# Cross-attention and FFN layers on one core: the router's product in 8 passes of 16 columns instead of 12 of 8

## What is computed

```
def _L1_ffn_ref(hidden_states, router_weight, sh_gate, sh_up, sh_down, r_gate, r_up, r_down):
    ...
    x = hidden_states.reshape(-1, H)
    logits = x.astype(jnp.float32) @ router_weight.astype(jnp.float32).T
    topk_vals, topk_idx = jax.lax.top_k(logits, TOP_K)
    topk_w = jax.nn.softmax(topk_vals, axis=-1)
    slot_mask = (topk_idx < NUM_LOCAL).astype(topk_w.dtype)
    comb_w = jnp.sum(topk_w * slot_mask, axis=-1).astype(x.dtype)
    shared = _mlp(x, sh_gate, sh_up, sh_down)
    routed = _mlp(x, r_gate, r_up, r_down) * comb_w[:, None]
    return (shared + routed).reshape(Bsz, Seq, H)
```

## Time and profile before

| | us |
|---|---|
| median of 3 runs | 455.13 |
| the 3 runs | 454.22, 456.38, 455.13 |
| the profiled execution | 456.1 |
| its span, first to last instruction | 454.4 |

### The profile page before, as it was taken

The page is one execution under the profiler, slowest core; times in us unless marked ns, Lnnn a source line. Parts: engine busy times, 40 slices in busy tenths (PEclk is TensorE's granted clock), DMA queues, the critical chain, the costliest instruction groups (busy, mean ns, idle before and its releaser), DMA issues.

```text
span 454.4 us, 8501 instructions
## 1 busy us (share of the span) xinstructions
PE 395.8 (87%) x3034; PEld 370.1 (81%) x3034; DVE 308.2 (68%) x929; ACT 226.6 (50%) x622; POOL 182.2 (40%) x300
## 2 busy tenths in 40 slices
PE   0668747699998999999989999999899989998596
PEld 0546636599987998899979997999789979996495
DVE  3479767796786666878765758878665666765343
ACT  0285564456564344656644345656543456564132
POOL 2235283734553433455434334545533332322031
PEclk9988986899999999999999999999999999999699
DMA  7997001000000001100000002000000000000000
GB/s 212 364 343 282 1 0 50 1 2 1 1 0 3 0 1 30 45 1 1 2 1 1 1 1 72 2 1 2 1 1 2 1 23 1 2 2 0 0 1 23
DMA packets 15080, 16.85 MB, mean 37 GB/s; under 512 B 1536, under 2 KB 14016, under 8 KB 15040
## 3 DMA queue, kind: packets, MB, share of 16 engines
q1 hardware_dynamic: 15040, 16.33, 11.1%
HBM read 15.28 MB, written 1.05 MB: 36 GB/s over the span
## 4 chain that ended last, share of the span: by engine, by line
PE 50%; DVE 24%; ACT 12%; POOL 6%; issue 5%; DMA 2%; SPq 1%; DVEq 0%; POOLq 0%; ACTq 0%
PE bank_s L300 13%; PE bank_u L300 10%; PE bank_qa L300 6%; ACT prob L741 6%; DVE prob L1326 5%; PE bank_o L300 4%; PE bank_pt L300 4%; PE bank_pt L471 3%; DVE pt_lo L1337 3%; DVE xn L1140 2%; POOL prob L1000 2%; DVE ut_lo L1343 2%; DMA wq_raw<-in_wqT 2%; ACT ut_hi L707 2%; PE bank_s L568 2%
## 5 line engine op out<-in xcount | busy, mean ns | idle before, releaser
L1000 POOL TENSOR_SCALAR prob<-prob,row_inv,valid_b 128x256 f32<-128x256 f32 x128 | 71.5, 567 | 84.2 <-DVE row_inv L1333 83.6
L741 ACT ACTIVATE prob<-prob,row_min 128x256 f32<-128x256 f32 x128 | 64.1, 502 | 71.5 <-DVE row_min L1326 71.5
L1337 DVE TENSOR_TENSOR pt_lo<-bank_pt,pt_hi 128x512 fp32r<-128x512 f32 x64 | 44.2, 690 | 14.1 <-ACT pt_hi L707 13.8
L1343 DVE TENSOR_TENSOR ut_lo<-bank_u,ut_hi 128x256 fp32r<-128x256 f32 x64 | 27.0, 422 | 38.6 <-ACT ut_hi L707 38.2
L1326 DVE CUSTOM_DVE_ANT_0 prob<-bank_s,masked 128x256 f32<-128x256 f32 x128 | 48.9, 419 | 2.9 <-PE bank_s L300 2.3
L300 PE MATMUL bank_u<-pt_hi,cx_hi 128*128 128x256 f32 x128 | 37.8, 295 | 7.0 <-DVE pt_lo L1337 6.7
L1012 POOL TENSOR_TENSOR act_lo<-act_raw,act_hi 128x256 fp32r<-128x256 f32 x32 | 24.0, 749 | 48.0 <-ACT act_hi L800 48.0
L300 PE MATMUL bank_o<-c_hi,ut_hi 128*128 128x256 f32 x128 | 39.2, 306 | 4.5 <-DVE ut_lo L1343 4.5
L707 ACT ACTIVATE pt_hi<-bank_pt 128x512 fp32r<-128x512 f32 x64 | 37.5, 586 | 10.8 <-PE bank_pt L471 10.8
L471 PE MATMUL bank_pt<-ident,prob 128*128 128x128 f32 x256 | 39.4, 277 | 3.9 <-POOL prob L1000 3.6
L300 PE MATMUL bank_qa<-xt_hi,a_hi 128*128 128x256 f32 x128 | 41.0, 320 | 0.8 <-DVE qa_lo L1315 0.7
(11 more groups left out here) (234 smaller groups left out, 1300.7 us busy)
## 6 DMA issues: line engine op xcount, KB each, us to landing
wq_raw<-in_wqT SPq DMA_DIRECT2D x4, 512.0 KB, 8.8
wo_raw<-in_wo SPq DMA_DIRECT2D x4, 512.0 KB, 9.7
w_raw<-in_w12T SPq DMA_DIRECT2D x1, 1408.0 KB, 9.1
gate_raw<-in_gateT SPq DMA_DIRECT2D x2, 576.0 KB, 8.8
up_raw<-in_upT SPq DMA_DIRECT2D x2, 576.0 KB, 10.5
down_raw<-in_downT SPq DMA_DIRECT2D x2, 576.0 KB, 12.4
x<-in_x SPq DMA_DIRECT2D x4, 256.0 KB, 5.3
guT<-in_guT SPq DMA_DIRECT2D x4, 256.0 KB, 6.8
```

What stands on the lines that cost most here:

```text
L741: last = act.activation(row, row, ACT.Exp, scale=-1.0, bias=row_min[:, h % 2, t:t + 1], accum_out=row_sum[:, h % 2, t:t + 1])
L1000: last = pool.tensor_scalar(row, row, row_inv[:, h % 2, t:t + 1], valid_b[:, 0:1], ALU.mult, ALU.mult)
L1337: dve.tensor_tensor(pt_lo[:, :, :].rearrange("p s t -> p (s t)"), bank["pt"][:, :], f32(pt_hi[:, :, :].rearrange("p s t -> p (s t)")), ALU ...
L1343: dve.tensor_tensor(ut_lo[:, :], bank["u"][:, 0:T], f32(ut_hi[:, :]), ALU.subtract).then_inc(S["u_l"], 1)
```

## The change

The two parts of the router's weights lie side by side in one tile, 8 columns of the high and 8 of the low. One pass multiplies a block of rows by all 16, so that a block needs two passes (its high and its low part) and not three; per batch 8 and not 12. The low by low product, left out before, is included. A row group's result has 16 columns in the bank: the sum of what met the high weights and the sum of what met the low. VectorE copies the first 8 to SBUF, adds the other 8, and takes the maxima from the sum. The NOP at that place is gone.

```diff
-        router_hi = sb("router_hi", [P, ND, NR], F32R)
-        router_lo = sb("router_lo", [P, ND, NR], F32R)
+        router = sb("router", [P, ND, 2, NR], F32R)
...
+        logits = sb("logits", [P, NT, NR])
...
                 for t in range(NT):
+                    cols = slice(t * P, (t + 1) * P)
                     for k in range(ND):
-                        cols = slice(t * P, (t + 1) * P)
-                        last = split_mm(bank["x1"][:, t * NR:(t + 1) * NR], yt_hi[:, k, cols], yt_lo[:, k, cols],
-                                        router_hi[:, k, :], router_lo[:, k, :], k == 0, k == ND - 1)
+                        for half in (yt_hi, yt_lo):
+                            last = pe.matmul(bank["x1"][:, t * 2 * NR:(t + 1) * 2 * NR], half[:, k, cols],
+                                             router[:, k, :, :].rearrange("p s n -> p (s n)"),
+                                             start=(k == 0 and half is yt_hi), stop=(k == ND - 1 and half is yt_lo),
+                                             skip_group_check=True)
                 last.then_inc(S["route_mm"], 1)
...
-            act.copy(router_hi[:, :, :], router_raw[:, :, :]).then_inc(S["router_hi"], 1)
+            act.copy(router[:, :, 0, :], router_raw[:, :, :]).then_inc(S["router_hi"], 1)
...
                 dve.wait_ge(S["route_mm"], b + 1)
-                hold()
-                for t in range(NT):
-                    last = dve.max(top8[:, t, :], bank["x1"][:, t * NR:(t + 1) * NR])
+                parts = bank["x1"][:, 0:NT * 2 * NR].rearrange("p (t s n) -> p s t n", s=2, n=NR)
+                link(dve.tensor_copy(top8[:, :, :], parts[:, 0, :, :]))
+                link(dve.tensor_tensor(logits[:, :, :], top8[:, :, :], parts[:, 1, :, :], ALU.add))
+                for t in range(NT):
+                    last = dve.max(top8[:, t, :], logits[:, t, :])
                 link(last)
...
-            dve.tensor_tensor(router_lo[:, :, :], router_raw[:, :, :], f32(router_hi[:, :, :]), ALU.subtract
+            dve.tensor_tensor(router[:, :, 1, :], router_raw[:, :, :], f32(router[:, :, 0, :]), ALU.subtract
                               ).then_inc(S["router_lo"], 1)
```

## The result

| | before | with the change |
|---|---|---|
| median | 456.38 | 458.37 |
| fastest run | 453.94 | 455.79 |
| profiled execution | 456.1 | 457.04 |
| its span | 454.4 | 455.1 |
| mean granted clock in it | 0.966 | 0.968 |

Both medians are of 13 runs on one chip; one run of each kernel (1309 and 2079 us) is left out of the comparison. The ratio is 1.0044, 95% interval 1.0022 to 1.0065. That is 2.0 us (458.37 - 456.38). It lies inside the 0.5% that the forecast called no change, but the interval leaves no doubt of its sign, and 458.37 lies above the forecast's range (453.3 to 456.9). Part of that distance, 1.25 us, is the kernel before itself, whose median was 455.13 in the three runs that the forecast started from. But a difference of 0.0 was forecast, and 2.0 came.

A forecast was written before the change was run, and what follows sets the result against it. TensorE, back to back, bounds the kernel, closely followed by a relay over VectorE, ScalarE and GpSimd. 3 x 0.15 - 0.45 = 0.0 us, so 455.1 against the 455.13 median (profiled 456.1); range 453.3 to 456.9.

The forecast's parts named there:

- The passes' price: TensorE's router: a 16-column pass costs 0.112 us like an 8-column one; four fewer save 0.45 us per batch.
- The wait at ffn_down(0): TensorE, batches 0 to 2: ffn_down(0) waits for chunk 0's act_lo; 0.04 of 0.45 us saved remain, 0.41 become wait.
- the hand-over: Time from the end of an act_lo on GpSimd to the matmul it releases on TensorE, taken as 0.14 us.
- VectorE's net 0.14: Batches 0 to 2: copy and add cost 0.40 us, a faster first difference gives time back; ffn_act(1) comes 0.14 later.
- an add that is not held: VectorE: the add, with one SBUF and one PSUM operand, runs free beside GpSimd; if held, net delay is 0.47 us.
- line 1387 free at 0.16: VectorE's first difference, formerly line 1381, starts after GpSimd's act_lo and lasts 0.16 us in all batches, not 0.42.
- ffn_down(1) and the sum of +0.15 per batch: TensorE, batches 0 to 2: ffn_down(1) starts 0.07 us later, restart loses 0.07 to 0.08; +0.15 carried to batch's end.
- no transfer, queue or wait of another engine is added: Last-batch part: the router's split at the start changes nothing and no further cost arises on other engines.
- the four rivals: All passes' gain kept, 453.3 (0.18); VectorE delay comes through, 455.9 to 456.1 (0.17); dearer passes, 458.7 (0.03); forecast itself (0.62).
- the chance of 0.92 for no change: Whole kernel: chance 0.92 that the time stays within some 0.5%, 2.3 us; 0.04 each for faster and slower.
- The first rival: TensorE, all batches: the whole 1.79 us comes off, 453.3; milder form, VectorE's addition hidden, 454.6; chance of either 0.18.
- the relay: What ffn_down waits for: work passed over VectorE, ScalarE and GpSimd; slack 0.04 us at ffn_down(0), 0.07 at ffn_down(1).

The follow-up runs named there:

- the pair with both relays free: Changed kernel, sums tile last, ternary tiles moved, ffn_act(0), act_lo(0) ahead, route_top behind ffn_act(1): 8 passes 453.71, ratio 0.9962; 12 passes, no copy and add, 455.57, 0.9990.
- the unplanned case: Changed kernel with sums tile last, ffn_act(0) ahead of the ternary residual, route_top behind ffn_act(1), transposes behind ffn_down(0): 456.03, ratio 0.9999 against before.

## Why the prediction was right or wrong

**The passes' price: right.** Eight passes of 16 columns take 0.91 us against 1.36 for 12 of 8, 0.114 each where 0.112 was taken. The 0.45 us per batch were confirmed by the pair with both relays free (0.43, 0.44, 0.32 and 0.47).

**The wait at ffn_down(0): right.** It starts 4.50 us after the first router matmul, against 4.53 forecast. One thing was not counted: the transposes wait too. The forecast had xn and TensorE arrive together (158.29 and 158.26) without the hand-over between them. In the change with old places the transposes come at 3.91, where 4.17 - 0.45 would be 3.72: some 0.19 us of wait, the 0.15 of the hand-over and a little more. It costs nothing, since the wait for `act_lo` behind it swallows it.

**VectorE's net 0.14: right, in each of its parts.** 0.20 between linked instructions, an add that is not held, and line 1387 free at 0.16. The rule on the shared port pair in the Trainium skill, "SBUF — State Buffer", Who interferes with whom, on instructions with two SBUF inputs held here and in the unplanned case as well (0.68 for line 1387 beside an `act_lo`). The forecast did say that line 1387 would last 0.16 in all four batches; in the last it now falls beside the `act_lo` of chunk 3, and takes 0.67:

```profile
438.46 0.67 DVE L1387 TENSOR_TENSOR top_d<-top 128x2 f32<-128x2 f32 x1
...
440.03 0.42 DVE L1372 SCALAR_TENSOR_TENSOR sig<-sig,bank_s 128x256 f32<-128x256 f32 x1 [0.83 <-ACT sig L808]
```

The 0.83 us of idle behind it show that nobody pays for it.

**ffn_down(1) and the sum of +0.15 per batch: right once the shift is taken out.** With the tiles in their old places 0.10, 0.19 and 0.15 us per batch, and -0.44 in the last; the sum is 0.0, and the run's median is 0.1 us above before.

**What failed** is the end of the part on the change: "no transfer, queue or wait of another engine is added", and under it the unspoken assumption that the passes that the diff doesn't name keep their 0.12 us. The diff adds a tile. The forecast went through all instructions that the change adds and removes and not through what it adds to memory. That term was missing from the sum altogether: it is 2.4 us by the run with the unused tile alone, and with the 0.1 of the change in its old places it makes the result of 2.0 within the intervals. None of the four rivals had it; the chance of 0.92 for no change happened to hold the result only because its bound is 2.3 us wide, and the range did not hold it. In the marks the shift is 0.42 to 0.47 us per batch by ffn_down(7) (22.55 against 22.13, 22.09 and 22.08) and 0.35 in the last batch, 1.7 of the 2.44 us by which the whole stretch is longer; the rest lies between these marks, attention for the most part.

**The first rival named a condition that is needed and not enough.** It asked for `act_lo` of chunk 0 to end 0.4 us earlier. With chunk 0 alone freed the gain was lost at ffn_down(1); when the relay of chunk 1 was freed too, it came off.

**What stays open.** Which of the two reads of a pass meets what, and why the place modulo 128 bytes matters: only 0 and 64 were tried, always with both operands whole multiples of 64, and no run tells the weights' read from the moving one. Why mix, scores and project moved by 1 ns where that place did not change, and why scores and project rose so little where it did. What makes the piece at the lower clock 6.8 or 10.2 us long. How much of the shift's 3.0 us of distances is hidden beside waits was not measured apart; 2.0 to 2.4 reach the time.

## What to carry to other kernels

A new tile is a change to every tile allocated behind it. Where TensorE runs back to back for most of the time, allocate a helper tile last, or compare the distances between passes of untouched products first; a mean duration that moves from 278 to 283 ns is enough to eat a gain. When passes are taken from an engine that is closely followed by a relay over other engines, look at how much slack the relay has: here it was 0.04 us, and the gain appeared only when the relay's instructions were moved ahead in all queues that they pass, and at its next chunk as well. A median can hold a longer piece at the lower clock that is not the price of the instructions added (1.2 of 1.67 us in the run with VectorE's work alone): a trace with marks tells the two apart.

## What the runs showed of the hardware that I had not expected

- Passes with 128 columns of weights and 256 moving columns in fp32r start 119.1 to 119.8 ns apart where both operands begin at the same place modulo 128 bytes of a partition, and 115.4 to 117.9 ns apart where they lie 64 bytes off. Shown in four families (gate and up, down, mix, ternary up), by moving tiles alone, three of them up and one down. It does not hold for all: scores and project with both operands at the same place took 118.8 and 118.3, and the ternary down products 118.8.
- Not only differences of two tiles are held by GpSimd: the pair of scalings that makes xn, which reads `x` and two small columns of statistics, took 1.14 us instead of 0.73 beside an `act_lo` of 0.74. The Trainium skill, "SBUF — State Buffer", Who interferes with whom, also lets instructions in VectorE's two-port fast modes take part in the lock. No run here settles whether these are such, but one of them lasts 0.41 us, as long as a subtraction of two tiles of that size (0.42), so no doubled rate shows.
- Between the end of xn on VectorE and the transposes that read it there are 0.15 us (156.98 and 157.13), as between the end of GpSimd's `act_lo` and its ffn_down (157.57 and 157.72).
